# Scores before turns in every round of an attention kernel, and the copies of the turned weights shared by two engines

## The reference

```
q = split_heads(x @ Wq.T); k = split_heads(x @ Wk.T); v = split_heads(x @ Wv.T)
a = einsum('bhnd,bhmd->bhnm', q, k) * D ** (-0.5) + 2 * adj[:, None]
a = where(any(a != 0, -1), a, -inf); p = softmax(a); p = where(isnan(p), 0, p)
o = einsum('bhnm,bhmd->bhnd', p, v)
out = layernorm(x + o @ Wo.T)
```

## Time and profile before

| | |
|---|---|
| median of 3 runs | 1979.76 us (1978.6 to 1979.77) |
| the profiled execution | 1979.87 us, its span 1977.9 us |
| PE busy | 1943.8 us, 98% of the span |
| DVE busy | 1476.5 us, 75% |
| ACT busy | 1491.0 us, 75% |
| POOL busy | 421.0 us, 21% |
| mean granted TensorE clock | 0.996 of full speed |

### The profile page before, as it was taken

One profiled execution on the slowest core, in us unless ns is written; L12 is line 12 of the kernel. 1 busy time (PEld: TensorE's weight loads), 2 busy tenths in 40 slices (PEclk: granted clock), 3 DMA queues, 4 the chain that ended last, 5 costly groups with the idle time before them and its releaser, 6 DMA issues. The chain is left out here.

```text
span 1977.9 us, 49324 instructions
## 1 busy us (share of the span) xinstructions
PE 1943.8 (98%) x16384; PEld 1604.8 (81%) x16384; DVE 1476.5 (75%) x6064; ACT 1491.0 (75%) x5393; POOL 421.0 (21%) x1291
## 2 busy tenths in 40 slices
PE   8999999999999999999999999999999999999995
PEld 6788888888888888888888888888888888888884
DVE  4778777877777787778777778877787777778775
ACT  6877778777777777777777777777777777777783
POOL 2122121222112221212221122212122211222103
PEclk9999999999999999999999999999999999999998
DMA  4120112211122101122111222011221111220101
GB/s 149 49 70 29 55 60 71 70 39 55 54 65 70 69 30 54 60 70 71 38 55 54 65 71 71 28 54 60 70 70 38 55 55 65 71 70 29 44 33 65
DMA packets 48637, 116.41 MB, mean 59 GB/s; under 512 B 5376, under 2 KB 5376, under 8 KB 44288
## 3 DMA queue, kind: packets, MB, share of 16 engines
q1 hardware_dynamic: 48384, 113.27, 17.0%
HBM read 79.69 MB, written 33.55 MB: 57 GB/s over the span
## 5 line engine op out<-in xcount | busy, mean ns | idle before, releaser
L500 ACT ACTIVATE e_sb<-neg_a,neg_max 128x128 f32<-128x128 f32 x2048 | 792.4, 389 | 110.2 <-DVE neg_max L615 110.2
L615 DVE CUSTOM_DVE_ANT_0 neg_a<-ps_s,adj_sb 128x128 f32<-128x128 f32 x2048 | 442.6, 286 | 353.9 <-PE ps_s L407 353.9
L338 PE MATMUL ps_w<-xt_hi,w_lo 128*128 128x512 f32 x1024 | 415.8, 406 | 9.0 <-DVE w_lo L569 7.1
L452 ACT ACTIVATE e_t<-ps_w 128x512 f32<-128x512 f32 x512 | 267.1, 599 | 204.8 <-PE ps_w L394 203.5
L339 PE MATMUL ps_w<-xt_lo,w_hi 128*128 128x512 f32 x1024 | 401.2, 392 | 0.0
L500 ACT ACTIVATION_READ_ACCUMULATOR e_sb<-neg_a,neg_max 128x1 f32 x2048 | 385.3, 188 | 0.0
L656 DVE SCALAR_TENSOR_TENSOR e_sb<-e_sb,r_inv 128x512 f32<-128x512 f32 x512 | 332.3, 690 | 9.2 <-DVE r_inv L652 0.5
L623 DVE TENSOR_REDUCE neg_min<-neg_a 128x16 f32<-128x2048 f32 x128 | 292.6, 2286 | 4.4
L276 POOL TENSOR_TENSOR xt_lo<-xt_raw,xt_hi 128x512 fp32r<-128x512 f32 x120 | 155.2, 1294 | 628.6 <-ACT xt_hi L452 628.6
L341 PE MATMUL ps_w<-xt_hi,w_hi 128*128 128x512 f32 x1024 | 274.9, 390 | 0.0
L394 PE MATMUL ps_w<-ident,e_sb 128*128 128x128 f32 x2048 | 262.4, 278 | 11.0 <-DVE x_sb L598 6.1
(11 more groups left out here) (56 smaller groups left out, 2495.8 us busy)
## 6 DMA issues: line engine op xcount, KB each, us to landing
x_sb<-x SPq DMA_DIRECT2D x32, 1024.0 KB, 4.9
out<-x_sb SPq DMA_DIRECT2D x128, 256.0 KB, 2.5
xt_raw<-xt SPq DMA_DIRECT2D x120, 256.0 KB, 2.9
adj_sb<-adj SPq DMA_DIRECT2D x32, 256.0 KB, 3.0
neg_a<-xt SPq DMA_DIRECT2D x4, 256.0 KB, 5.5
v_sb<-wk SPq DMA_DIRECT2D x4, 256.0 KB, 6.4
e_sb<-wq SPq DMA_DIRECT2D x4, 256.0 KB, 7.1
v_sb<-wv SPq DMA_DIRECT2D x4, 256.0 KB, 7.8
```

The costliest lines, as they stand in the source:

```text
L338: pe.matmul(out, lhs_lo(c), rhs_hi(c), start=(c == 0), stop=False)
L452: return act.activation(out, in_, ACT.Copy, scale=scale)
L500: last = act.activation(e_sb[:, i, h, :], neg_a[:, i, h, :], ACT.Exp, scale=-1.0, bias=neg_max[:, i, h:h + 1], accum_out=sums[:, i, h:h + 1])
L615: last = dve.tensor_tensor_reduce(out=neg_a[:, i, h, :], in0=ps_s[h][:, i * NODES:(i + 1) * NODES], in1=adj_sb[:, g % PAIR, i, :], scale=- ...
```

## The change

It does three things. On PE the scores of a round now stand ahead of the turns of the round before; values follow the turns directly, then the projections as before. The copies of the turned quads are split: ACT copies quads 0 and 2, DVE copies quads 1 and 3 (the new `turned_out` in the vector program, between values_lo and the doubling and bias), and the single semaphore turned_copied becomes even_copied and odd_copied, for which PE waits by the parity of the quad.

```diff
@@ the tensor engine's helpers and loop
+            def wait_turned(f, i):
+                if i % 2:
+                    pe.wait_ge(odd_copied, 2 * f + i // 2 + 1)
+                else:
+                    pe.wait_ge(even_copied, 2 * f + i // 2 + 1)
@@ def wait_bank(u)
                     if kind == "t":
-                        pe.wait_ge(turned_copied, n)
+                        wait_turned(g, index)
@@ def values(f)
                 for i in range(GG):
-                    pe.wait_ge(turned_copied, count("t", f, i))
+                    wait_turned(f, i)
@@ the loop over the rounds
             for f in range(PHASES + 1):
-                if f:
-                    turn(f - 1)
                 if f < PHASES:
                     scores(f)
                 if f:
+                    turn(f - 1)
                     values(f - 1)
@@ the scalar engine, def turned_out(f)
-                for i in range(GG):
+                for i in range(0, GG, 2):
...
-                         ).then_inc(turned_copied, 1)
+                         ).then_inc(even_copied, 1)
@@ the vector engine
+            def turned_out(f):
+                for i in range(1, GG, 2):
+                    if f:
+                        dve.wait_ge(values_done, f)
+                    else:
+                        dve.wait_ge(xt_lo_done, CH)
+                    dve.wait_ge(turned, count("t", f, i))
+                    dve.tensor_copy(e_t[:, i].rearrange("p a b -> p (a b)"), ps_w[USE["t", f, i] % BANKS][:, :]
+                                    ).then_inc(odd_copied, 1)
@@ the vector engine's loop
                 if f > 1:
                     values_lo(f - 2)
+                if f:
+                    turned_out(f - 1)
                 if f % TILES == TILES - 1 and f + 1 < PHASES:
                     double_adj(f // TILES + 1)
                 bias(f)
@@ after the loop
             values_lo(PHASES - 2)
+            turned_out(PHASES - 1)
             values_lo(PHASES - 1)
```

More of the change, by code:

```diff
@@ L172, in build @@
         turned = sem("turned")
-        turned_copied = sem("turned_copied")
+        even_copied = sem("even_copied")
+        odd_copied = sem("odd_copied")
         values_done = sem("values_done")
```

## The result

The changed kernel takes 2032.24 us, the median of 4 runs (2031.55 to 2034.68), against 1979.67 us for the kernel before (1978.6 to 1979.77). The ratio is 1.027 with a 95% interval of 1.0256 to 1.0284: slower by 52.6 us. The profiled execution took 2034.68 us, so its terms sum to some 2 us more than the medians differ by. The forecast was 2025, in a range of 1998 to 2040.

What follows compares the result with a forecast made beforehand. PE's own program was taken as the bound. Terms +0.20, +0.20 and -0.015 make +0.385 us a round; over 122 rounds +47, less 2.3 at the ends, +44.7 on 1979.87: 2025 us, range 1998 to 2040.

Steps and rivals of the forecast that it cites:

- both mechanisms: On PE each round: a fourth array-mode change, +0.20 us, and values waiting for the last quad's copy, +0.20 us.
- the middle: The 122 undisturbed rounds between start and end, claimed to cost +0.385 us each, +47 us together.
- One more change of mode: On PE each round: four array-mode seams summing to 0.75 us in place of three summing to 0.55, so +0.20.
- The drains: PE's delay over pace at a mode change: 0.09 us from turns to scores, 0.11 from scores to whole array.
- scores to whole array: PE's seam from scores into turns, priced from round 0's scores to projections: 0.11 + 0.11 = 0.22 us.
- The last quad of values: Values on PE wait 0.18 us for DVE's copy of the fourth quad, plus 0.02 for its load: +0.20 a round.
- choosing between 0.431 and 0.66: Time of DVE's quad copy from PSUM: 0.66 us taken from PSUM rows, over 0.431 for a copy from SBUF.
- Banks inside turns: Turns on PE wait 0.03 us less for a bank in half the rounds: -0.015 us a round.
- DVE in time: After an o projection, DVE is free for the second quad's copy by 0.1 us; busy share rises to about 84%.
- Ends: First and last two rounds, bound by DVE: -1.3 us in round 127, about -0.5 twice at the start; -2.3 together.
- the scores need only q and k: DVE step: exponentials, reduction, scaling and turns move up to 1.2 us later, while scores do not wait for them.

Runs made afterwards that it cites:

- experiment 4: The kernel before with values moved behind the first projection in 120 of the rounds, no copy split; 2007.52 us, ratio 1.0144.
- experiment 6: The changed kernel with DVE copying only 256 of the fourth quad's 512 columns, the rest left out, so values use old weights there; 1998.55 us, ratio 1.0097.
- experiment 1: The kernel before with only PE's order changed to scores, turns, values; ACT still copies all four quads; 2021.26 us, ratio 1.021.
- experiment 5: The changed kernel with PE taking turns ahead of scores, the old order, in rounds 2 and 3 only; 2029.01 us, ratio 1.0247.
- experiment 3: The changed kernel with values moved behind the first projection in rounds 4 to 123; 2020.48 us, ratio 1.0207.
- experiment 7: The kernel before with the first quad of turns, its bank use and ACT copy moved ahead of the last projection in rounds 3 to 123; 1982.44 us, ratio 1.0012.

## Why the prediction was right, and where its sizes were off

The direction, the bound (PE's own program) and both mechanisms held. That the middle came within 1.3 us is in part luck: of its two large terms one was 0.05 too high and the other 0.07 too low. By term, measured as means over the middle of the traces:

- *One more change of mode*: +0.20 forecast, +0.15 measured. The drains came as read, 0.09 each. The step that was off is scores to whole array, which I took from scores to projections: the second turn comes after 0.164, 0.055 over its pace, where behind a change the second projection pass is 0.11 late. A projection there does cost the full price (experiment 4, +0.227 a round with the second drain in it).
- *The last quad of values*: +0.20 forecast, +0.27 measured (0.265 in experiment 6). The copy takes 0.69, not 0.66, but PE's load for it goes 2.92 after the turns' start in the mean, close to the 2.90 forecast. The miss is on the other side: since the turns' load was cheaper than taken, values start at 2.00 and not at 2.04, and reach the quad some 0.05 sooner. The wait is 0.24, and its load 0.02 to 0.03. In choosing between 0.431 and 0.66 the PSUM rows were the right ones, and the Trainium skill's rule (VectorE: DVE Perf Modes, Why PSUM operands drop a tier) now has a row for a copy, which agrees with it: 256 columns 424 ns, 512 columns 691 or 692, so 1.04 ns a column, against 431 ns for 512 columns from SBUF.
- *Banks inside turns*: -0.015 forecast, -0.02 measured.
- *DVE in time*: right. In the round shown the second quad's copy followed values_lo without a gap and ended before the fourth quad was turned.
- *Ends*: -2.3 forecast, wrong in sign. The last full turns to the end of the span are 58.98 us before and 57.05 after (1975.75 to 2032.8), -1.9. But at the start turns of round 1 to those of round 4 take 45.5 (44.24 to 89.71) in place of 39.4 (41.79 to 81.22), +6.0, and the first turns now stand behind the scores of round 1 and a seam, +1.2. (Another 1.2 of the two spans' difference lies ahead of the first scores, 18.79 against 20.04, in loads that the change does not touch.) The step that failed said "the scores need only q and k", and priced the start by DVE's loop alone. In rounds 1 and 2, q is copied last; the scores at the head of rounds 2 and 3 wait for it and hold up the turns behind them, and the granted clock falls to half within the first wait and again behind the second.

The middle: 122 rounds at +0.396 are +48.3, forecast +47. Nearly the whole miss of 7 us is the start. That q's copy is what scores wait for rests on four scores that start 0.10 or 0.11 us behind its end, in the changed kernel and in experiment 1, and on experiment 5. How much the start costs in an execution other than the profiled one stays open: experiment 5 gains 5.3 us there by the profiles, and 3.2 by the medians.

## What to carry to other kernels

On an engine that is always busy, price an order by its seams: count the changes of array mode, and for each the drain and the first load that nothing hides. Then, for every operand that moves next to its producer, set the time that its copy is ready beside the time it is wanted; and count such a wait from where the weight load could start, not from the matmul: what looked like 0.05 us for a bank cost 0.15. Where a small wait on a buffer recurs each round, look for a buffer that stands idle just then before changing the order, and price the short first and last rounds by themselves.

## What the runs showed of the hardware that was not expected

- A wait for a PSUM bank held the weight load as well as the pass: in experiment 3 the load started at 1011.75 with its pass, where it could have started with the last turn, as in experiment 7 (1016.88). The cost was 0.15 us, although no mode changed and the pass was only 0.05 later than the pace of turns.
- Behind row strips the first whole-array turn delays the second by 0.055 us, a projection pass by 0.11 us.
- The granted clock was 0.50 of full (1.2 of 2.4 GHz) in the turns of round 2 of the changed kernel, which followed a wait of 2.59 us and scores, and 1.00 in the same rounds where PE was idle for at most 1.24 us at a time (experiment 5). It was also 1.00 behind a wait of 2.05 us and 0.50 behind the next, of 2.57 (experiment 1).
